# Two causal attentions: heads stacked on one set of 64 array rows instead of two row halves

## The chip, the cores and the metric

One core of a Trainium2 chip runs the whole program. TensorE (PE) multiplies, VectorE (DVE) reduces and copies, ScalarE (ACT) exponentiates, GpSimd (POOL) masks and issues the loads, SyncE (SP) issues stores. The metric is the device time of one execution in microseconds (us); lower is better. The kernel before took 5852.48 us (median of three runs, 5826.07 to 5913.86).

## The reference

Two layers over a (2, 2048, 256) input, each "x = layernorm(x + block(x))": a causal grouped attention (16 heads of 16 numbers, 4 key/value heads), a top-2 mixture of 8 experts, an attention with low-rank keys and values and rotary positions (16 heads, masked by pages of 64), and a block of two local-attention layers with gated units. The part that matters is the softmax attention over all 2048 positions:

```python
att = jnp.einsum('bsgmd,btgd->bgmst', q, k) / scale
att = jnp.where(causal, -jnp.inf, att)
att = jax.nn.softmax(att, axis=-1)
ctx = jnp.einsum('bgmst,btgd->bsgmd', att, v).reshape(b, s, DIM)
```

The second global attention computes the same with its own keys for each head and with `pages[None, :] <= pages[:, None]` as the mask.

## The kernel before, in words

The program runs stages one after another, named by the first letter of their tiles: Z clears buffers, A projects, **B is the first global attention**, C its output, then routing and E the experts, F combines and projects, **G is the second global attention** and H its output, and I, J, K are the local layers, each run twice. One function, `attention`, makes both B and G.

`attention` runs 8 iterations (2 batches of 4 groups); an iteration handles 4 heads. Queries and keys are kept split into a high and a low part, so that a product of 16 numbers keeps its precision: in `qs` and `ks` each head has three groups of 16 rows (high times high, low times high, high times low), 48 rows in all. Heads 0 and 2 lie in rows 0 to 47 and heads 1 and 3 in rows 64 to 111, that is, in the two halves of the array's 128 rows. Two more rows (48, 49 and 112, 113) hold the negated row maximum, split high and low, against ones in `ks`.

Each iteration does two things, interleaved:

- **Pieces** (line 419): for a block of 128 queries the scores against up to 512 keys are made in one of three PSUM buffers `pm` (RING), and DVE takes their maximum (509). On the diagonal a matmul against a mask (415) comes first. When the pieces of a chunk of 512 queries are done, DVE folds the maxima (515), POOL splits them in two (328, 330), PE turns them (409), ACT negates them (483), and SP writes them by DMA into `qs` (354). There are 144 pieces, in 160 matmuls.
- **Steps** (40 in an iteration, for 4 chunks of 512 queries by 128 keys each): four score matmuls (458) in two pairs, heads 0 and 1 and heads 2 and 3, over 48 + 2 rows; ACT takes the exponential of each pair (495); POOL masks on the diagonal (303); and PE weights the values of the step before with it (435), four heads side by side in 32 columns each.

The queues' order is written out by hand: the list `ring` holds pieces, folds and turns in order, `cut` deals some 3.8 of its events to each step, 22 steps ahead of the scores that need them (AHEAD), and the rest, 83 events, comes as an opening before the first iteration. In a step PE runs score pair 1, an event, score pair 2, an event, the weighting of the step before, and the other events. POOL loads the next iteration's `qs`, `ks` and `v` at step 4 (290 to 292).

Of the kernel before, what the change touches and what calls it, by code (L numbers as in the profile page):

```python
# [6 lines left out]
F32 = mybir.dt.float32  # L7
F32R = mybir.dt.float32r
# [169 lines left out]

def attention(nc, sem, tag, nk, page, qh, ql, kh, kl, vs, mask_qk, ident_bf, ident, ot):

    R = 3 * HD
    PAR = GRP // 2
    NA = max(1, nk // 2)
    RING = 3
    AHEAD = 22

# [5 lines left out]
    for qb in range(NQ):  # L192
        full, rest = divmod((qb + 1) * P, CH)
        for kc in range(full + (rest > CH // 2)):
            pieces += [(qb, kc, min(CH, (qb + 1) * P - kc * CH), [h]) for h in range(GRP)]
        if 0 < rest <= CH // 2:
            pieces += [(qb, full, rest, [u, u + 2]) for u in range(2)]
    NP = len(pieces)
    steps = [(qc, kb) for qc in range(NC4) for kb in range(SUB * (qc + 1))]
    NS = len(steps)  # L200
# [1 line left out]
    ring = []  # L202
    for j in range(NP):
        ring.append(("piece", j, 0))
        for behind, kind in ((1, "fold"), (4, "turn")):
            for c in range(NC4):
                if (closes[c] + behind) % NP == j:
                    ring.append((kind, c, (closes[c] + behind) // NP))
# [16 lines left out]

    with ExitStack() as ctx:
        sb = lambda n, s, t: ctx.enter_context(nc.sbuf_tensor(tag + n, s, t))
        qs = [sb(f"qs{i}", [P, NC4, PAR, CH], F32R) for i in range(2)]
        ks = [sb(f"ks{i}", [P, NA, S], F32R) for i in range(2)]
        v = [sb(f"v{i}", [P, NQ, nk, VW], F32) for i in range(2)]  # L230
        p = sb("p", [P, 2, GRP, CH], F32)
        o = sb("o", [P, 2, CH], F32)
        mpart = sb("mpart", [P, 2, PAR, NQ, NC4], F32)
        mfold = sb("mfold", [P, 2, PAR, SUB], F32)
        m = sb("m", [P, P], F32R)
        mrow = sb("mrow", [2 * GRP * SUB, P], F32)
        one = sb("one", [2, CH], F32)
# [20 lines left out]

            return sum(kb >= SUB * qc for qc, kb in steps[:t])

        LOADS = 2 * 6 + 1
        CONSTS = 3 + 4

        def all_iterations(eng, body):

# [11 lines left out]
        def _(pool):  # L277
# [3 lines left out]
            pool.dma_start(idf[:], ident).then_inc(c_in, 16)  # L281

            def load(i, s):
                q_rows = lambda a: a[ds(i * (GRP * HD), GRP * HD), :].rearrange("(a b e) (c t) -> b e c a t", b=2, e=HD, t=CH)
                k_rows = lambda a, u: (a[ds(i * HD, HD), :].unsqueeze(1) if nk == 1 else
                                       a[ds(i * (GRP * HD), GRP * HD), :].rearrange("(a b e) t -> b e a t", b=2, e=HD)[u])
                for u in range(2):
                    for r, (a, c) in enumerate(((qh, kh), (ql, kh), (qh, kl))):
                        rows = slice(64 * u + r * HD, 64 * u + (r + 1) * HD)
                        pool.dma_start(qs[s][rows].bitcast(F32), q_rows(a)[u]).then_inc(q_in[s], 16)  # L290
                        pool.dma_start(ks[s][rows].bitcast(F32), k_rows(c, u)).then_inc(q_in[s], 16)
                pool.dma_start(v[s][:], vs[ds(i * S, S), :].rearrange("(kb p) (h e) -> p kb h e", p=P, e=VW)
                               ).then_inc(q_in[s], 16)

# [15 lines left out]
            load(0, 0)  # L310
            pool.wait_ge(ready, 2)
            for s in range(2):
                for u in range(2):
                    pool.dma_start(ks[s][64 * u + R:64 * u + R + 2].bitcast(F32).rearrange("r a (c t) -> r (a c) t", t=CH),
                                   one[:].unsqueeze(1).to_broadcast([2, NA * NC4, CH])).then_inc(c_in, 16)
            load(1, 1)

            def split(k, e, clears):
                kind, c, late = ring[e]
                if kind != "fold":  # L320
                    return
                if clears is not None:
                    wait_apart(pool, cleared, clears, fence)
                wait_apart(pool, folded, (k - late) * NC4 + c + 1, fence)
                wait_apart(pool, mt_done, (k - late) * NC4 + c, fence)
                parts = m[:, 0:2 * GRP * SUB].rearrange("p (b r n) -> p r b n", b=2, r=2)
                whole = mfold[:].rearrange("p b a j -> p b (a j)")
# [19 lines left out]
        @block.sync  # L347
        def _(sp):
            def m_row(k, e, s):
                _, c, late = ring[e]  # L350
                sp.wait_ge(mr_done, (k - late) * NC4 + c + 2)
                s = (s + late) % 2
                for u in range(2):
                    sp.dma_start(qs[s][64 * u + R:64 * u + R + 2, c].bitcast(F32).rearrange("r a (j t) -> r (a j) t", t=P),
                                 mrow[u * GRP * SUB:(u + 1) * GRP * SUB]).then_inc(m_in, 16)

            def out(i, c):
                sp.wait_ge(o_done, i * NC4 + c + 2)
                sp.dma_start(ot[ds(i * P, P), c * CH:(c + 1) * CH], o[:, c % 2]).then_inc(o_out[c % 2], 16)

            for k, e in opening:
                if ring[e][0] == "turn":
                    m_row(k, e, 0)

            def body(i, s, half):
                for t, (qc, kb) in enumerate(steps):
                    for e in range(cut[t], cut[t + 1]):
                        if ring[e % NE][0] == "turn" and exists(i + e // NE, e % NE):
                            m_row(i + e // NE, e % NE, (s + e // NE) % 2)
                    if kb == 0:  # L370
                        if qc:
                            out(i, qc - 1)
                        elif not static(i, 0):
                            out(i - 1, NC4 - 1)
            all_iterations(sp, body)
            out(NIT - 1, NC4 - 1)
            for c in range(2):
                sp.wait_ge(o_out[c], 16 * (NC4 // 2 * NIT) + 1)

        @block.tensor  # L380
        def _(pe):
# [19 lines left out]
            def event(k, e, s):  # L401
# [13 lines left out]
                    pe.matmul(t[:, 0:c * w].rearrange("p (h k) -> p h k", k=w)[:, :, w - P:w], idb[:],  # L415
                              mqk[:].unsqueeze(1).to_broadcast([P, c, P]), start=True, stop=False, skip_group_check=True)
                for n, h in enumerate(heads):
                    rows = slice(64 * (h % 2), 64 * (h % 2) + R)
                    last = pe.matmul(t[:, n * w:(n + 1) * w],  # L419
                                     qs[s][rows, qb // SUB, h // 2, qb % SUB * P:(qb % SUB + 1) * P],  # L420
                                     ks[s][rows, h // 2 % NA, kc * CH:kc * CH + w], start=not diag, stop=True,
                                     skip_group_check=diag)
                last.then_inc(s_max, 1)

# [15 lines left out]
            def body(i, s, half):  # L440
                for t, (qc, kb) in enumerate(steps):
                    off = max(0, kb - SUB * qc) * P
                    events = [(e // NE, e % NE) for e in range(cut[t], cut[t + 1]) if exists(i + e // NE, e % NE)]
                    if kb == 0:
                        pe.wait_ge(m_in, (i * NC4 + qc + 1) * 32 + 1)

                    def some(a, z):
                        for n in range(a, min(z, len(events))):
# [5 lines left out]
                    for pr in range(2):  # L454
                        pe.wait_ge(e_done[pr], i * NS + t + 1)
                        for h in (2 * pr, 2 * pr + 1):
                            rows = slice(64 * (h % 2), 64 * (h % 2) + R + 2)
                            score = pe.matmul(psc[:, h, off:CH], ks[s][rows, h // 2 % NA, kb * P:(kb + 1) * P],  # L458
                                              qs[s][rows, qc, h // 2, off:CH], start=True, stop=True)
                        score.then_inc(s_done, 1)  # L460
                        some(pr, pr + 1)
                    if t:
                        weigh(i, s, t - 1)
                    elif not static(i, 0):
                        weigh(i - 1, 1 - s, NS - 1)
                    some(2, len(events))

            pe.wait_ge(c_in, 16 * CONSTS)
            pe.wait_ge(q_in[0], 16 * LOADS)
# [6 lines left out]
        def _(act):  # L476
            def m_rows(k, e):
                kind, c, late = ring[e]
                if kind != "turn":
                    return  # L480
                act.wait_ge(mt_done, (k - late) * NC4 + c + 2)
                act.wait_ge(m_in, (k - late) * (NC4 * 32) + c * 32 + 1)
# [19 lines left out]
        def _(dve):  # L502
            def event(k, e):
                kind, j, late = ring[e]
                if kind == "piece":
                    qb, kc, w, heads = pieces[j]
                    dve.wait_ge(s_max, k * NP + j + 2)
                    a = heads[0] // 2
                    dve.tensor_reduce(mpart[:, heads[0] % 2, a:a + len(heads), qb, kc],  # L509
                                      pm[slots[e]][:, 0:len(heads) * w].rearrange("p (h k) -> p h k", k=w),  # L510
                                      AX, ALU.max).then_inc(max_done, 1)
                elif kind == "fold":
                    dve.wait_ge(max_done, (k - late) * NP + closes[j] + 2)
                    dve.wait_ge(m_all, (k - late) * NC4 + j + 1)
                    dve.tensor_reduce(mfold[:].rearrange("p b a j -> p (b a) j"),
                                      mpart[:, :, :, j * SUB:(j + 1) * SUB].rearrange("p b a q k -> p (b a) q k"),
                                      AX, ALU.max).then_inc(folded, 1)

            def copy_out(i, qc):
# [1824 lines left out]
```

## Time and profile before

| | |
|---|---|
| median of 3 runs (lowest, highest) | 5852.48 us (5826.07, 5913.86) |
| profiled execution, its own time | 5825.77 us |
| its span, mean granted clock | 5824.2 us, 0.851 |
| B, from PE's first instruction to its last | 149.6 to 1187.3, 1037.7 us |
| G, likewise | 2553.3 to 3620.5, 1067.2 us |

The engines overlap, so busy shares do not add up. A matmul's recorded time holds its latency, so two that follow each other overlap in the record; how fast they follow is read from the difference of their starts. Two matmuls whose starts lie 0.004 us apart run side by side. The granted clock, PEclk, is a share of 2.4 GHz: 1.00 is that level, 0.50 is 1.2 GHz, and what lies between is a mean over both.

### The profile page before, as it was taken

To read this page: it belongs to the slowest core of one execution; us is meant where nothing else is said; L and a number is where in the kernel's file an instruction comes from. 1 tells how busy PE (TensorE), PEld (TensorE's weight loads), DVE (VectorE), ACT (ScalarE), POOL (GpSimd) and SP (SyncE) were. 2 spreads that over 40 slices of the span, in tenths; PEclk is the share of its full clock that TensorE was granted. 3 is DMA by queue.
4 is the path that set the end of the run, shared out by engine and by line. 5 is a ranking of instruction groups with operands and counts; after the bars stand their busy time and mean duration, and the time that the engine had idled before them with its cause. 6 is when DMAs were issued, how large, how long until landed. Compare 5 with 4: busy or idle time off the path is not lost. (4 is left out here: it accounts for less than half of the span.)

```text
span 5824.2 us, 81282 instructions
## 1 busy us (share of the span) xinstructions
PE 4707.0 (81%) x25828; PEld 3020.7 (52%) x25828; DVE 3059.5 (53%) x5338; ACT 2344.9 (40%) x3695; POOL 861.0 (15%) x1228
## 2 busy tenths in 40 slices
PE   4999999952999993759999998476997967699787
PEld 2444434341887882323434343355775755577566
DVE  1777767632344442746667674475443547444354
ACT  1365555521344441204555555133443423334333
POOL 1011211115000004010111110132111003211100
PEclk8698889875999996856778898698998989899888
DMA  7111221023112112350333220334332123333211
GB/s 213 25 27 27 35 40 29 11 96 114 48 47 75 46 44 85 130 103 9 49 47 50 38 40 22 120 118 133 111 118 78 33 60 118 125 118 110 73 43 33
DMA packets 271929, 413.90 MB, mean 71 GB/s; under 512 B 40836, under 2 KB 178945, under 8 KB 268028
## 3 DMA queue, kind: packets, MB, share of 16 engines
q0 software_dynamic: 64160, 224.28, 16.3%
q1 hardware_dynamic: 202844, 181.40, 9.7%
q8 instruction: 173, 2.83, 0.2%
q10 hardware_dynamic: 4608, 4.20, 0.2%
q14 instruction: 144, 1.18, 0.1%
HBM read 252.70 MB, written 156.19 MB: 70 GB/s over the span
## 5 line engine op out<-in xcount | busy, mean ns | idle before, releaser
L509 DVE TENSOR_REDUCE G_mpart<-G_pm 128x1 f32<-128x512 f32 (+3 forms) x1152 | 705.1, 656 | 340.3 <-PE G_pm L419 331.0
L509 DVE TENSOR_REDUCE B_mpart<-B_pm 128x1 f32<-128x512 f32 (+3 forms) x1152 | 704.4, 656 | 300.0 <-PE B_pm L419 290.4
L495 ACT ACTIVATE G_p<-G_psc 128x1024 f32<-128x1024 f32 (+3 forms) x640 | 544.1, 894 | 470.5 <-PE G_psc L458 469.7
L495 ACT ACTIVATE B_p<-B_psc 128x1024 f32<-128x1024 f32 (+3 forms) x640 | 543.1, 894 | 445.2 <-PE B_psc L458 444.6
L419 PE MATMUL G_pm<-G_ks,G_qs 48*128 48x512 f32 (+3 forms) x1280 | 523.5, 521 | 8.9 <-DVE G_mpart L509 4.3
L419 PE MATMUL B_pm<-B_ks,B_qs 48*128 48x512 f32 (+3 forms) x1280 | 510.3, 507 | 9.4 <-DVE B_mpart L509 4.1
L458 PE MATMUL G_psc<-G_qs,G_ks 50*128 50x512 f32 (+3 forms) x1280 | 357.9, 453 | 16.0 <-issue 13.4
L419 PEld LDWEIGHTS G_pm<-G_ks,G_qs 48*128 48x128 f32 x1280 | 231.4, 224 | 265.1 <-DVE G_mpart L509 171.4
L435 PE MATMUL G_po<-G_p,G_v 128*32 128x512 f32 (+3 forms) x2560 | 359.4, 639 | 6.7 <-DVE G_o L523 6.0
L419 PEld LDWEIGHTS B_pm<-B_ks,B_qs 48*128 48x128 f32 x1280 | 226.2, 218 | 259.3 <-DVE B_mpart L509 175.0
L458 PE MATMUL B_psc<-B_qs,B_ks 50*128 50x512 f32 (+3 forms) x1280 | 347.3, 440 | 10.0 <-issue 7.4
L435 PE MATMUL B_po<-B_p,B_v 128*32 128x512 f32 (+3 forms) x2560 | 348.1, 620 | 8.4 <-DVE B_o L523 6.6
L1017 PE MATMUL E_pO<-E_wp,E_a 128*128 128x256 f32 (+1 forms) x1920 | 255.2, 298 | 57.9 <-DVE E_a L1079 52.3
L1050 ACT ACTIVATE E_hs<-E_pH,E_bf 128x512 f32<-128x512 f32 (+1 forms) x192 | 115.7, 602 | 434.9 <-PE E_pG L1004 434.9
L1818 DVE TENSOR_REDUCE J_mx<-J_pS 128x8 f32<-128x2048 f32 x64 | 146.7, 2292 | 262.2 <-PE J_pS L1710 262.2
L1017 PEld LDWEIGHTS E_pO<-E_wp,E_a 128*128 128x128 f32 (+1 forms) x1920 | 250.0, 200 | 63.1 <-DVE E_a L1079 57.2
L1004 PE MATMUL E_pH<-E_xT,E_wfg 128*128 128x512 f32 (+1 forms) x1152 | 259.7, 362 | 19.7 <-DVE E_wfg L1089 15.6
L1004 PE MATMUL E_pG<-E_xT,E_wfg 128*128 128x512 f32 (+1 forms) x1152 | 255.1, 357 | 0.0
L1564 POOL TENSOR_TENSOR I_t<-I_qn,I_R 128x512 f32<-128x512 f32 x128 | 167.8, 1332 | 510.5 <-DVE I_qn L1618 510.5
L1726 PEld LDWEIGHTS J_pO<-J_v,J_pT 128*128 128x128 f32 x2048 | 239.6, 193 | 3.2
L1726 PE MATMUL J_pO<-J_v,J_pT 128*128 128x65 f32 x2048 | 236.5, 274 | 0.0
L1004 PEld LDWEIGHTS E_pH<-E_xT,E_wfg 128*128 128x128 f32 x1152 | 195.6, 193 | 55.4 <-issue 21.8
(308 smaller groups left out, 7879.6 us busy)
## 6 DMA issues: line engine op xcount, KB each, us to landing
J_v<-lve POOLq DMA_DIRECT2D x64, 520.0 KB, 4.2
J_k<-lkT POOLq DMA_DIRECT2D x64, 512.0 KB, 5.1
lve<-I_v SPq DMA_DIRECT2D x64, 260.0 KB, 2.1
lqT<-I_tT SPq DMA_DIRECT2D x64, 256.0 KB, 2.4
lkT<-I_tT SPq DMA_DIRECT2D x64, 256.0 KB, 2.6
J_q<-lqT POOLq DMA_DIRECT2D x64, 256.0 KB, 4.2
ein<-Z_z SPq DMA_DIRECT2D x8, 1228.0 KB
E_xin<-ein POOLq DMA_DIRECT2D x8, 1152.0 KB, 6.4
```

The lines of the kernel that those rows point to most:

```text
L419: last = pe.matmul(t[:, n * w:(n + 1) * w], qs[s][rows, qb // SUB, h // 2, qb % SUB * P:(qb % SUB + 1) * P], ks[s][rows, h // 2 % NA, kc * ...
L435: last = pe.matmul(po[VW * h:VW * (h + 1), off:CH], v[s][:, kb, h % nk], p[:, t % 2, h, off:CH], start=kb == 0, stop=kb == SUB * (qc + 1) - 1,
L458: score = pe.matmul(psc[:, h, off:CH], ks[s][rows, h // 2 % NA, kb * P:(kb + 1) * P], qs[s][rows, qc, h // 2, off:CH], start=True, stop=True)
L495: act.activation(p[:, t % 2, 2 * pr:2 * pr + 2, off:CH], psc[:, 2 * pr:2 * pr + 2, off:CH], ACT.Exp, scale=SC).then_inc(e_done[pr], 1)
L509: dve.tensor_reduce(mpart[:, heads[0] % 2, a:a + len(heads), qb, kc], pm[slots[e]][:, 0:len(heads) * w].rearrange("p (h k) -> p h k", k=w) ...
L1004: last = pe.matmul(bank[ht % 2][:, 0:w], wfg_p[pw][:, i, kc, ht * P:(ht + 1) * P], xT[px][:, kc, 0:w], start=kc + j == 0, stop=kc == KC - ...
L1017: last = pe.matmul(pO[j // 2][0:r, j % 2 * D:(j % 2 + 1) * D], a[pa][:, ht, j * P:j * P + r], wp_p[pw][:, ht], start=ht + i == 0, stop=ht ...
L1050: act.activation(hs[:, ht % 2, 0:w], pH[ht % 2][:, 0:w], ACT.Identity, bias=bf[:, s, ht:ht + 1]).then_inc(hs_done, 1)
L1564: last = pool.tensor_tensor(t2[:, u, :, :, a:a + H], qn[:, u, :, :, z:z + H], R[:, :, ds(w_, 1), a:a + H].to_broadcast([P, 2, LH, H]), ALU ...
L1726: last = pe.matmul(pO[h // HB][:, h % HB * VE:(h % HB + 1) * VE], pT[:, r, i, s], v[:, u, s, h * VE:(h + 1) * VE], start=s == 0, stop=s == 1)
L1818: dve.tensor_reduce(mx[:, u], pS[:], AX, ALU.max).then_inc(m_done, 1)
```

## The change

All four products of the split halves are now stacked, high-high, high-low, low-high and low-low, in 64 rows, and every head uses rows 0 to 63 of the array. The maximum's two rows are 64 and 65, so a score matmul reads rows 0 to 65. Pieces that hold two heads take neighbours (0 and 1, 2 and 3). The turn of the maxima comes 12 pieces after its chunk's last piece, not 4. In a step the weighting follows score pair 2 directly, and the event that stood there comes behind it. An iteration's load is 21 DMAs instead of 13, and the maxima are written by one DMA instead of two. Semaphore counts follow.

```diff
-    R = 3 * HD
-    PAR = GRP // 2
-    NA = max(1, nk // 2)
+    R = 4 * HD
...
-            pieces += [(qb, full, rest, [u, u + 2]) for u in range(2)]
+            pieces += [(qb, full, rest, [u, u + 1]) for u in (0, 2)]
...
-        for behind, kind in ((1, "fold"), (4, "turn")):
+        for behind, kind in ((1, "fold"), (12, "turn")):
...
-                for u in range(2):
-                    for r, (a, c) in enumerate(((qh, kh), (ql, kh), (qh, kl))):
-                        rows = slice(64 * u + r * HD, 64 * u + (r + 1) * HD)
-                        pool.dma_start(qs[s][rows].bitcast(F32), q_rows(a)[u]).then_inc(q_in[s], 16)
-                        pool.dma_start(ks[s][rows].bitcast(F32), k_rows(c, u)).then_inc(q_in[s], 16)
+                for r, (a, c) in enumerate(((qh, kh), (qh, kl), (ql, kh), (ql, kl))):
+                    rows = slice(r * HD, (r + 1) * HD)
+                    for h in range(GRP):
+                        pool.dma_start(qs[s][rows, :, h].bitcast(F32), a[ds(i * (GRP * HD) + h * HD, HD), :]
+                                       .rearrange("e (c t) -> e c t", t=CH)).then_inc(q_in[s], 16)
+                    pool.dma_start(ks[s][rows].bitcast(F32), c[ds(i * (nk * HD), nk * HD), :].rearrange("(h e) t -> e h t", e=HD)
+                                   ).then_inc(q_in[s], 16)
...
-                for u in range(2):
-                    sp.dma_start(qs[s][64 * u + R:64 * u + R + 2, c].bitcast(F32).rearrange("r a (j t) -> r (a j) t", t=P),
-                                 mrow[u * GRP * SUB:(u + 1) * GRP * SUB]).then_inc(m_in, 16)
+                sp.dma_start(qs[s][R:R + 2, c].bitcast(F32).rearrange("r a (j t) -> r (a j) t", t=P),
+                             mrow[:]).then_inc(m_in, 16)
...
-                    rows = slice(64 * (h % 2), 64 * (h % 2) + R)
                     last = pe.matmul(t[:, n * w:(n + 1) * w],
-                                     qs[s][rows, qb // SUB, h // 2, qb % SUB * P:(qb % SUB + 1) * P],
-                                     ks[s][rows, h // 2 % NA, kc * CH:kc * CH + w], start=not diag, stop=True,
+                                     qs[s][0:R, qb // SUB, h, qb % SUB * P:(qb % SUB + 1) * P],
+                                     ks[s][0:R, h % nk, kc * CH:kc * CH + w], start=not diag, stop=True,
...
-                            rows = slice(64 * (h % 2), 64 * (h % 2) + R + 2)
-                            score = pe.matmul(psc[:, h, off:CH], ks[s][rows, h // 2 % NA, kb * P:(kb + 1) * P],
-                                              qs[s][rows, qc, h // 2, off:CH], start=True, stop=True)
+                            score = pe.matmul(psc[:, h, off:CH], ks[s][0:R + 2, h % nk, kb * P:(kb + 1) * P],
+                                              qs[s][0:R + 2, qc, h, off:CH], start=True, stop=True)
                         score.then_inc(s_done, 1)
-                        some(pr, pr + 1)
+                        if pr == 0:
+                            some(0, 1)
...
-                    some(2, len(events))
+                    some(1, len(events))
```

What PE runs in one step of stage B in which nothing is masked, before (458 scores, 419 pieces, 435 weighting; the number behind a tile is its buffer):

```order
L458 MATMUL B_psc<-B_qs0,B_ks0 128x512 x2
L419 MATMUL B_pm2<-B_ks0,B_qs0 128x512
L458 MATMUL B_psc<-B_qs0,B_ks0 128x512 x2
L419 MATMUL B_pm0<-B_ks0,B_qs0 128x512
L435 MATMUL B_po<-B_p,B_v0 32x512 x4
```

and in such a step now (451 scores, 413 pieces, 429 weighting):

```order
L451 MATMUL B_psc<-B_qs0,B_ks0 128x512 x2
L413 MATMUL B_pm1<-B_ks0,B_qs0 128x512
L451 MATMUL B_psc<-B_qs0,B_ks0 128x512 x2
L429 MATMUL B_po<-B_p,B_v0 32x128 x4
L413 MATMUL B_pm2<-B_ks0,B_qs0 128x512
L413 MATMUL B_pm0<-B_ks0,B_qs0 128x512
L413 MATMUL B_pm1<-B_ks0,B_qs0 128x512
```

The instructions are the same in number and size; the piece ahead of the weighting has moved behind it, and three now stand there in a row. Not in these rows: before, neighbours took the array's two halves in turn, and now all take its lower rows.

The load that POOL issues for one iteration, at the start of stage B, before:

```order
L290 DMA B_qs<-qh 16x8x512
L291 DMA B_ks<-kh 16x2048
L290 DMA B_qs<-ql 16x8x512
L291 DMA B_ks<-kh 16x2048
L290 DMA B_qs<-qh 16x8x512
L291 DMA B_ks<-kl 16x2048
L290 DMA B_qs<-qh 16x8x512
L291 DMA B_ks<-kh 16x2048
L290 DMA B_qs<-ql 16x8x512
L291 DMA B_ks<-kh 16x2048
L290 DMA B_qs<-qh 16x8x512
L291 DMA B_ks<-kl 16x2048
```

and now:

```order
L285 DMA B_qs<-qh 16x4x512 x4
L287 DMA B_ks<-kh 16x2048
L285 DMA B_qs<-qh 16x4x512 x4
L287 DMA B_ks<-kl 16x2048
L285 DMA B_qs<-ql 16x4x512 x4
L287 DMA B_ks<-kh 16x2048
L285 DMA B_qs<-ql 16x4x512 x4
L287 DMA B_ks<-kl 16x2048
L289 DMA B_v<-vs 128x16x32
```

Queries come head by head, half as much in each DMA, and a fourth product is loaded; the load of `v` follows in both.

## Rows read from the trace of the kernel before

**Rows 1.** The page: span, engine totals, and PE's busy tenths and clock in 40 slices

```profile
span 5824.2 us, 81282 instructions
PE 4707.0 (81%) x25828; PEld 3020.7 (52%) x25828; DVE 3059.5 (53%) x5338; ACT 2344.9 (40%) x3695; POOL 861.0 (15%) x1228
PE   4999999952999993759999998476997967699787
PEclk8698889875999996856778898698998989899888
```

**Rows 2.** Busy time of each engine, clock, DMA: stages B and G, first to last PE instruction

```profile
149.60:1187.30 1037.70, 989.58 (x5536) 417.20 (x5536) 723.45 (x1216) 548.81 (x672) 140.62 (x270) 0.83 0.17 27
2553.30:3620.50 1067.20, 1019.61 (x5536) 428.44 (x5536) 724.25 (x1216) 551.11 (x673) 98.47 (x270) 0.80 0.23 37
```

**Rows 3.** Who waited for whom: us in total, times, longest us

```profile
ACT B_p L495 <- PE B_psc L458: 444.6, 346, 21.3
DVE B_mpart L509 <- PE B_pm L419: 290.4, 354, 29.2
PE B_pm L409 <- POOL B_m L330: 11.4, 10, 1.3
PE G_pm L409 <- POOL G_m L330: 8.8, 10, 1.2
```

**Rows 4.** Timeline of PE in stage B at the full clock: start, us, instruction, count

```profile
806.08 0.51 PE L419 MATMUL B_pm<-B_ks,B_qs 48*128 48x512 f32 x2
806.43 0.63 PE L458 MATMUL B_psc<-B_qs,B_ks 50*128 50x512 f32 x4
806.90 0.40 PE L419 MATMUL B_pm<-B_ks,B_qs 48*128 48x512 f32 x1
807.23 1.06 PE L435 MATMUL B_po<-B_p,B_v 128*32 128x512 f32 x8
808.22 0.50 PE L419 MATMUL B_pm<-B_ks,B_qs 48*128 48x512 f32 x2
```

**Rows 5.** Timeline of PE in stage E (experts), all 128 rows, full clock

```profile
1644.50 1.56 PE L1004 MATMUL E_pH<-E_xT,E_wfg 128*128 128x512 f32 x6
1645.89 1.56 PE L1004 MATMUL E_pG<-E_xT,E_wfg 128*128 128x512 f32 x6
```

**Rows 6.** Timeline of PE in stage B at half the clock

```profile
787.36 0.63 PE L458 MATMUL B_psc<-B_qs,B_ks 50*128 50x512 f32 x2
787.92 0.40 PE L415 MATMUL B_pm<-B_mqk,B_idb 128*128 128x256 bf16 x1
788.24 0.58 PE L419 MATMUL B_pm<-B_ks,B_qs 48*128 48x256 f32 x1
...
790.45 1.93 PE L435 MATMUL B_po<-B_p,B_v 128*32 128x512 f32 x8
792.31 0.79 PE L419 MATMUL B_pm<-B_ks,B_qs 48*128 48x512 f32 x2
792.90 0.63 PE L458 MATMUL B_psc<-B_qs,B_ks 50*128 50x512 f32 x2
793.33 0.62 PE L419 MATMUL B_pm<-B_ks,B_qs 48*128 48x512 f32 x1
...
796.37 0.23 PE L415 MATMUL B_pm<-B_mqk,B_idb 128*128 128x128 bf16 x1
```

**Rows 7.** Busy times as in rows 2, of stretches at one clock each

```profile
149.60:198.00 48.40, 46.50 (x109) 22.51 (x109) 38.93 (x67) 0.53 (x2) 0.82 (x4) 0.50 0.40 46
198.00:230.00 32.00, 31.34 (x119) 14.00 (x122) 22.24 (x38) 10.96 (x15) 2.95 (x6) 0.50 0.03 9
776.00:782.50 6.50, 5.24 (x38) 2.32 (x36) 4.64 (x9) 2.81 (x6) 1.69 (x4) 1.00 0.01 3
792.00:796.20 4.20, 4.20 (x20) 1.64 (x16) 2.48 (x4) 1.94 (x2) 0.00 (x0) 0.50 0.02 4
806.00:826.00 20.00, 19.71 (x127) 8.31 (x127) 16.36 (x28) 14.60 (x17) 1.05 (x3) 1.00 0.01 2
```

**Rows 8.** POOL's timeline: a load in stage B, and the mask after it

```profile
851.15 0.58 POOL L290 DMA_DIRECT2D B_qs<-qh  x1 [0.20 <-issue]
851.77 0.51 POOL L291 DMA_DIRECT2D B_ks<-kh  x1
...
870.71 0.63 POOL L303 TENSOR_SCALAR_AFFINE_SELECT B_p<-B_p 128x512 f32<-128x512 f32 x1 [10.05 <-ACT B_p L495]
```

More of the change, by code:

```diff
@@ L227, in attention @@
         sb = lambda n, s, t: ctx.enter_context(nc.sbuf_tensor(tag + n, s, t))
-        qs = [sb(f"qs{i}", [P, NC4, PAR, CH], F32R) for i in range(2)]
-        ks = [sb(f"ks{i}", [P, NA, S], F32R) for i in range(2)]
+        qs = [sb(f"qs{i}", [P, NC4, GRP, CH], F32R) for i in range(2)]
+        ks = [sb(f"ks{i}", [P, nk, S], F32R) for i in range(2)]
         v = [sb(f"v{i}", [P, NQ, nk, VW], F32) for i in range(2)]
@@ L232, in attention @@
         o = sb("o", [P, 2, CH], F32)
-        mpart = sb("mpart", [P, 2, PAR, NQ, NC4], F32)
-        mfold = sb("mfold", [P, 2, PAR, SUB], F32)
+        mpart = sb("mpart", [P, GRP, NQ, NC4], F32)
+        mfold = sb("mfold", [P, GRP, SUB], F32)
         m = sb("m", [P, P], F32R)
@@ L259, in masked @@
             return sum(kb >= SUB * qc for qc, kb in steps[:t])
-        LOADS = 2 * 6 + 1
-        CONSTS = 3 + 4
+        LOADS = 4 * (GRP + 1) + 1
+        CONSTS = 3 + 2
         def all_iterations(eng, body):
@@ L283, in load @@
             def load(i, s):
-                q_rows = lambda a: a[ds(i * (GRP * HD), GRP * HD), :].rearrange("(a b e) (c t) -> b e c a t", b=2, e=HD, t=CH)
-                k_rows = lambda a, u: (a[ds(i * HD, HD), :].unsqueeze(1) if nk == 1 else
-                                       a[ds(i * (GRP * HD), GRP * HD), :].rearrange("(a b e) t -> b e a t", b=2, e=HD)[u])
-                for u in range(2):
-                    for r, (a, c) in enumerate(((qh, kh), (ql, kh), (qh, kl))):
-                        rows = slice(64 * u + r * HD, 64 * u + (r + 1) * HD)
-                        pool.dma_start(qs[s][rows].bitcast(F32), q_rows(a)[u]).then_inc(q_in[s], 16)
-                        pool.dma_start(ks[s][rows].bitcast(F32), k_rows(c, u)).then_inc(q_in[s], 16)
+                for r, (a, c) in enumerate(((qh, kh), (qh, kl), (ql, kh), (ql, kl))):
[5 more added lines that the diff above has]
+                                   ).then_inc(q_in[s], 16)
                 pool.dma_start(v[s][:], vs[ds(i * S, S), :].rearrange("(kb p) (h e) -> p kb h e", p=P, e=VW)
@@ L312, in _ @@
             for s in range(2):
-                for u in range(2):
-                    pool.dma_start(ks[s][64 * u + R:64 * u + R + 2].bitcast(F32).rearrange("r a (c t) -> r (a c) t", t=CH),
-                                   one[:].unsqueeze(1).to_broadcast([2, NA * NC4, CH])).then_inc(c_in, 16)
+                pool.dma_start(ks[s][R:R + 2].bitcast(F32).rearrange("r a (c t) -> r (a c) t", t=CH),
+                               one[:].unsqueeze(1).to_broadcast([2, nk * NC4, CH])).then_inc(c_in, 16)
             load(1, 1)
@@ L325, in split @@
                 wait_apart(pool, mt_done, (k - late) * NC4 + c, fence)
-                parts = m[:, 0:2 * GRP * SUB].rearrange("p (b r n) -> p r b n", b=2, r=2)
-                whole = mfold[:].rearrange("p b a j -> p b (a j)")
+                parts = m[:, 0:2 * GRP * SUB].rearrange("p (r n) -> p r n", r=2)
+                whole = mfold[:].rearrange("p a j -> p (a j)")
                 pool.tensor_copy(parts[:, 0], whole).then_inc(m_hi, 1)
@@ L352, in m_row @@
                 s = (s + late) % 2
-                for u in range(2):
-                    sp.dma_start(qs[s][64 * u + R:64 * u + R + 2, c].bitcast(F32).rearrange("r a (j t) -> r (a j) t", t=P),
-                                 mrow[u * GRP * SUB:(u + 1) * GRP * SUB]).then_inc(m_in, 16)
+                sp.dma_start(qs[s][R:R + 2, c].bitcast(F32).rearrange("r a (j t) -> r (a j) t", t=P),
+                             mrow[:]).then_inc(m_in, 16)
             def out(i, c):
@@ L444, in body @@
                     if kb == 0:
-                        pe.wait_ge(m_in, (i * NC4 + qc + 1) * 32 + 1)
+                        pe.wait_ge(m_in, (i * NC4 + qc + 1) * 16 + 1)
                     def some(a, z):
@@ L481, in m_rows @@
                 act.wait_ge(mt_done, (k - late) * NC4 + c + 2)
-                act.wait_ge(m_in, (k - late) * (NC4 * 32) + c * 32 + 1)
+                act.wait_ge(m_in, (k - late) * (NC4 * 16) + c * 16 + 1)
                 act.activation(mrow[:], pm[slots[e]][0:2 * GRP * SUB, 0:P], ACT.Copy, scale=-1.0).then_inc(mr_done, 1)
@@ L507, in event @@
                     dve.wait_ge(s_max, k * NP + j + 2)
-                    a = heads[0] // 2
-                    dve.tensor_reduce(mpart[:, heads[0] % 2, a:a + len(heads), qb, kc],
+                    dve.tensor_reduce(mpart[:, heads[0]:heads[-1] + 1, qb, kc],
                                       pm[slots[e]][:, 0:len(heads) * w].rearrange("p (h k) -> p h k", k=w),
@@ L514, in event @@
                     dve.wait_ge(m_all, (k - late) * NC4 + j + 1)
-                    dve.tensor_reduce(mfold[:].rearrange("p b a j -> p (b a) j"),
-                                      mpart[:, :, :, j * SUB:(j + 1) * SUB].rearrange("p b a q k -> p (b a) q k"),
+                    dve.tensor_reduce(mfold[:],
+                                      mpart[:, :, j * SUB:(j + 1) * SUB],
                                       AX, ALU.max).then_inc(folded, 1)
```

## The prediction

> **What bounds the kernel now.** I read the page first: PE is recorded busy for 81% of the span, more than any other engine, and its slices are nearly all 9s, while the clock row wanders between 5 and 9 [rows 1]. The change touches only the two global attentions, B and G, so the next view is the windows over them: 1037.7 and 1067.2 us, 2104.9 together, with PE in work for 95% of it, DVE for some 70%, ACT for 53%, at a mean clock of 0.83 and 0.80 [rows 2]. The waits say the same from the other side: ACT waits 444.6 us in B for scores from PE and DVE 290.4 us for pieces, while what PE itself waits for is small [rows 3]. So in B and G the end is set by how fast PE gets through its list, and that hangs on three things: whether matmuls run side by side, what a change of layout costs, and the clock.
>
> *Side by side.* At the full clock four score matmuls of 512 columns start at 806.43 and the next instruction at 806.90: 0.47 us for four, 0.235 for a pair [rows 4]. In E, where each uses all 128 rows, six take 1.39 us, 0.232 each [rows 5]. A pair in two row halves costs what one alone costs. The same holds for a piece beside a score of the other half.
>
> *Changes of layout.* I call it a change when PE goes from one way of using the array (a row half, all rows, four column strips) to another. Piece to weighting takes 0.33 (806.90 to 807.23), 0.10 over the plain 0.233; and the first pair behind a weighting takes 0.35 until the next, 0.115 more than a pair: its weights load in the open [rows 4]. At half the clock a pair takes 0.43 (792.90 to 793.33), scores to mask 0.56, so 0.13 for the change, and the first pair behind a weighting 0.59, so 0.16 for the weights [rows 6]. The weighting takes 0.99 to the next start at the full clock, 1.86 at half: 0.89 and 1.73 without its change [rows 4, 6].
>
> **What the edits cost.** The instructions stay the same. What goes is the pairing, and what comes is changes of layout: scores now read rows 0 to 65, across the half boundary, so I take them to use the array whole, as the mask matmuls do, while pieces on rows 0 to 63 remain a half. Counted over the program's order, one iteration of B has 167 changes before and 248 now; on 172 of them (76 into scores, 96 into pieces) a full set of weights loads in the open.
>
> Per iteration there are 28 steps with 512 columns and four each with 384, 256 and 128, which is 34 full ones: 136 full-size score matmuls, 136 piece matmuls (the same triangle), 34 weightings and 8192 mask columns. A mask of 256 columns takes 0.32 less 0.13 [rows 6], so these are 6.1 us at half the clock and about 3.0 at full.
>
> - At half the clock: 272 x 0.43 = 117.0; 34 x 1.73 = 58.8; masks 6.1; 248 x 0.13 = 32.2; 172 x 0.16 = 27.5. Sum 241.6, times 8 iterations 1933 us.
> - At the full clock: 272 x 0.233 = 63.4; 34 x 0.89 = 30.3; masks 3.0; 248 x 0.10 = 24.8; 172 x 0.115 = 19.8. Sum 141.3, times 8 is 1130, and 1150 with the opening at half the clock as now [rows 7].
>
> Both are above today's 1052 mean: the attentions get slower at either level, and the clock decides by how much. DVE (723 us) and ACT (549) fit under either sum [rows 2].
>
> **The clock.** In B it was at half for the opening and beyond, 149.6 to 230, though PE was in work for 46.5 of 48.4 and 31.3 of 32.0 us: busy alone did not bring it up [rows 7]. It fell after a thin stretch around a diagonal (776 to 782.5, narrow matmuls, PE in work for 5.24 of 6.50), and rose after 792 to 796.2, where two piece-score pairs, another pair and two weightings of 512 columns stood close [rows 6, 7]. What preceded the rise was the array in use in both halves at once, next to weightings that fill it. After the change nothing but masks, turns and weightings uses more than rows 0 to 65; at half the clock a full step becomes 8 x 0.43 + 1.73 + 5 x 0.13 + 4 x 0.16 = 6.5 us, with eight matmuls one by one, where it is 4.06 now (792.31 to 796.37). The thin stretches at the diagonals stay and get thinner. I conclude that the clock still falls, and that the stretches that raised it no longer exist: it stays at half nearly throughout. By the Trainium skill (TensorE: Matmul & The Clock Gate, "What's actually happening") sustained work releases the gate and only idleness closes it; by that rule the changed attentions would run at the full clock. Rows 7 speak against it for half-filled arrays.
>
> Each tenth of the work done at the full clock returns (1933 - 1130) / 10 = 80 us per attention. I take one tenth: 1853 us each. The bounds are none and three tenths.
>
> **The other edits.** The turn's later place removes at most the 11.4 and 8.8 us that PE waits for POOL there [rows 3]; I take all, -20. Its maxima are needed at steps 12 and 24 and turned at steps 5 and 21, the tightest with three steps to spare, some 10 us or more: no new wait. The piece behind the weighting costs no extra change; it is in the counts. Eight more loads at 0.55 us [rows 8] stand before PE's first instruction: 4.4 us each and some landing, +10 for both; zero and +40 are the bounds. Inside the iterations POOL issues 21 for 13, some 14 us for 9, with the next mask 19.6 us after the first issue today and later in a slower kernel [rows 8]: covered by four steps. Were the mask late all the same, it would be by 14 - 9 = 5 us at most, in 6 loads of each attention: 60 us, an upper bound. One DMA for the maxima instead of two saves SP 0.6 us off PE's path: nothing.
>
> Sum: 2 x 1853 - 2105 = +1601, -20, +10: +1591. Against the profiled execution's 5825.77 that is **7420 us**; the median of the runs shown is 27 above that execution, well inside my range.
>
> **The rivals.**
> - *The clock recovers in each iteration.* If undivided scores count like full-array work, stretches of scores next to a weighting can bring it up, and half the work runs fast: 1933 - 400 = 1530 each, in all 6770; with less of it up to 7250. For it speaks that E's work, on all rows, runs at the full clock [rows 5]; against it, that scores fill only 66 rows.
> - *The full clock throughout*, as in 806 to 826 today [rows 7]: 1150 each, +195 - 10, in all 6010. For it: PE gets denser in time, with no gaps. Against: the opening.
> - *Faster: changes cost nothing.* If rows 0 to 63 and rows 0 to 65 count as one layout and the full clock holds, only the 80 changes around weightings remain: 63.4 + 30.3 + 3.0 + 8.0 + 4.6 = 109.3, 895 per attention with the opening, in all 5510. It decides in step for step between scores and pieces: at full clock the kernel breaks even when a change with its weights costs 0.13 on average, and the rows give 0.10 + 0.115 x 172 / 248 = 0.18. The Trainium skill (TensorEngine Tiling (Array Packing), "Key Properties") says that changing the tiling mode drains TensorE, and the trace agrees with 0.10 to 0.13 [rows 4, 6]. At half the clock it would lose even with free changes: (117.0 + 58.8 + 6.1) x 8 = 1455.
>
> **Chances.** Half the clock nearly throughout 0.67 (7250 to 7600); recovering in part 0.15 (6650 to 7250); full clock 0.13; free changes 0.03; something between that ends within 2% 0.02. About 2% (117 us) is what the runs can tell from no change. The range 6650 to 7620 leaves out the last three. Faster 0.03, same 0.02, slower 0.95.
>
> **What would show it.** The changed profile should have B and G near 1850 us with a mean clock near 0.55 or less; scores of a pair 0.43 apart and not 0.004; 0.56 from a score pair to its piece; DVE and ACT with the same work over a longer time; turns without a wait for POOL; all other stages as long as now. I am wrong if the clock row shows 8s and 9s in B and G (then 6010), or if scores and pieces follow each other without the extra 0.1. Nothing here rests on other stages.

## The result, and the profile after

The changed kernel took 7660.23 us (median of four runs, 7629.05 to 7670.92) against 5853.6 before: a ratio of 1.3098, with a 95% interval of 1.303 to 1.3166. Forecast were 7420 and a range of 6650 to 7620. The direction and the mechanism held; the size was short by 240 us, and the time lies 40 above the range. Medians here are over all executions and ratios over the fast ones alone, which matters in experiment 3, where two of four were slow (6304.73, the profiled one, and 6376.31 us).

The page of the changed kernel, the lines that answer to [rows 1]:

```profile
span 7668.6 us, 81462 instructions
PE 6607.0 (86%) x25828; PEld 3738.6 (49%) x25828; DVE 3110.4 (41%) x5338; ACT 2400.7 (31%) x3695; POOL 917.2 (12%) x1352
PE   5999999999936999567999999999667979669967
PEclk7555555555568999785555555555688989879988
```

PE executes as many instructions as before. The clock row is a flat 5 over both attentions, slices 2 to 11 and 19 to 28, counted from 1. The windows over them, and over parts of them (columns as in [rows 2]):

```profile
151.20:2115.80 1964.60, 1961.25 (x5536) 780.74 (x5536) 748.27 (x1215) 577.08 (x672) 163.68 (x318) 0.50 0.10 15
3496.30:5441.30 1945.00, 1934.96 (x5536) 770.48 (x5536) 748.29 (x1216) 578.06 (x673) 121.47 (x318) 0.51 0.16 24
...
200.00:2115.80 1915.80, 1912.60 (x5428) 756.57 (x5427) 708.86 (x1148) 576.55 (x670) 162.85 (x314) 0.50 0.09 14
3496.30:5404.00 1907.70, 1898.59 (x5312) 756.88 (x5312) 747.58 (x1214) 547.96 (x637) 119.63 (x312) 0.50 0.17 24
5404.00:5441.30 37.30, 36.37 (x228) 13.60 (x224) 0.70 (x2) 30.10 (x36) 1.84 (x6) 1.00 0.02 9
```

B and G take 3909.6 us together where they took 2104.9 [rows 2]: +1805 of the span's +1844. From 200 us to the end of B PE is in work for 1912.6 of 1915.8 us, and its granted clock never leaves half. DVE and ACT do the same work as before, in busy times 3 to 5% longer. The clock comes up once, at 5404 in G, when no pieces are left; ahead of it the timeline of PE shows only scores, weightings and one turn:

```profile
5396.63 2.08 PE L451 MATMUL G_psc<-G_qs,G_ks 66*128 66x512 f32 x4
5398.64 1.94 PE L429 MATMUL G_po<-G_p,G_v 128*32 128x512 f32 x8
...
5402.30 1.94 PE L429 MATMUL G_po<-G_p,G_v 128*32 128x512 f32 x8
```

The missing pieces alone do not explain it: B's last piece starts by 2037, and the same scores and weightings to its end at 2115.8 stay at half the clock.

The waits, which answer to [rows 3] (who waited for whom: us, times, longest us):

```profile
ACT B_p L489 <- PE B_psc L451: 1309.3, 589, 17.0
DVE B_mpart L502 <- PE B_pm L413: 1163.6, 704, 30.6
```

Both engines wait for PE three to four times as long as before, and at the turns PE no longer waits for POOL: those lines are gone.

PE's timeline in stage B, at half the clock, which answers to [rows 6]:

```profile
1043.73 1.65 PE L413 MATMUL B_pm<-B_ks,B_qs 64*128 64x512 f32 x3
1045.30 1.22 PE L451 MATMUL B_psc<-B_qs,B_ks 66*128 66x512 f32 x2
1046.33 0.33 PE L410 MATMUL B_pm<-B_mqk,B_idb 128*128 128x128 bf16 x1
1046.59 0.79 PE L413 MATMUL B_pm<-B_ks,B_qs 64*128 64x512 f32 x1
1047.31 1.22 PE L451 MATMUL B_psc<-B_qs,B_ks 66*128 66x512 f32 x2
1048.46 1.94 PE L429 MATMUL B_po<-B_p,B_v 128*32 128x512 f32 x8
1050.33 0.29 PE L410 MATMUL B_pm<-B_mqk,B_idb 128*128 128x128 bf16 x1
```

Each price of the prediction can be read off it. Three pieces until the scores: 1.57, that is 3 x 0.43 + 0.16 + 0.13. Two scores until the mask: 1.03, that is 2 x 0.43 + 0.16, with no change between them, since both use the whole array. One piece until the scores: 0.72, that is 0.43 + 0.16 + 0.13. Two scores until the weighting: 1.15, 0.13 more than 1.02. The weighting: 1.87, as before. Nothing runs side by side.

### The profile page after: what moved, and what is told of

It reads as the page before. It is cut to its first block and busy times, and to the rows that moved or that the text cites. A ratio compares the mean times of both kernels' runs of the same rounds, so it can differ in the third digit from the quotient of the medians.

```text
span 7668.6 us, 81462 instructions
## 1 busy us (share of the span) xinstructions
PE 6607.0 (86%) x25828; PEld 3738.6 (49%) x25828; DVE 3110.4 (41%) x5338; ACT 2400.7 (31%) x3695; POOL 917.2 (12%) x1352
## 5 line engine op out<-in xcount | busy, mean ns | idle before, releaser
L413 PE MATMUL G_pm<-G_ks,G_qs 64*128 64x512 f32 (+3 forms) x1280 | 751.7, 670 | 0.2 <-DVE G_mpart L502 0.2
L413 PE MATMUL B_pm<-B_ks,B_qs 64*128 64x512 f32 (+3 forms) x1280 | 751.7, 670 | 0.1
L451 PE MATMUL B_psc<-B_qs,B_ks 66*128 66x512 f32 (+3 forms) x1280 | 689.4, 647 | 2.9 <-issue 2.9
L451 PE MATMUL G_psc<-G_qs,G_ks 66*128 66x512 f32 (+3 forms) x1280 | 676.8, 635 | 9.4 <-issue 8.9
L413 PEld LDWEIGHTS B_pm<-B_ks,B_qs 64*128 64x128 f32 x1280 | 343.6, 304 | 407.7 <-issue 267.3
L413 PEld LDWEIGHTS G_pm<-G_ks,G_qs 64*128 64x128 f32 x1280 | 343.6, 304 | 407.7 <-issue 267.3
L429 PE MATMUL B_po<-B_p,B_v 128*32 128x512 f32 (+3 forms) x2560 | 537.5, 933 | 0.3 <-POOL B_p L300 0.3
L429 PE MATMUL G_po<-G_p,G_v 128*32 128x512 f32 (+3 forms) x2560 | 523.6, 910 | 0.4 <-POOL G_p L304 0.3
L451 PEld LDWEIGHTS B_psc<-B_qs,B_ks 66*128 66x128 f32 x1280 | 322.7, 312 | 303.8 <-issue 294.7
L451 PEld LDWEIGHTS G_psc<-G_qs,G_ks 66*128 66x128 f32 x1280 | 313.3, 304 | 298.9 <-issue 276.2
```

The source lines that it names most:

```text
L413: last = pe.matmul(t[:, n * w:(n + 1) * w], qs[s][0:R, qb // SUB, h, qb % SUB * P:(qb % SUB + 1) * P], ks[s][0:R, h % nk, kc * CH:kc * CH ...
L429: last = pe.matmul(po[VW * h:VW * (h + 1), off:CH], v[s][:, kb, h % nk], p[:, t % 2, h, off:CH], start=kb == 0, stop=kb == SUB * (qc + 1) - 1,
L451: score = pe.matmul(psc[:, h, off:CH], ks[s][0:R + 2, h % nk, kb * P:(kb + 1) * P], qs[s][0:R + 2, qc, h, off:CH], start=True, stop=True)
```

## The experiments

All were timed against the kernel before on the same chip; a ratio is to that kernel. "B" and "G" are the two attentions' windows of the profiled execution, from PE's first instruction to its last.

**1. Filling the rows of the scores.** Two theories stood: that the clock stays down because matmuls that run one by one fill half the rows (theory 1), or because of the rhythm with its pauses at 248 changes of layout (theory 2). Edit on the changed kernel:

```diff
+            for t in (*qs, *ks):
+                dve.memset(t[64:P].bitcast(F32), 0.0)
...
-                            score = pe.matmul(psc[:, h, off:CH], ks[s][0:R + 2, h % nk, kb * P:(kb + 1) * P],
-                                              qs[s][0:R + 2, qc, h, off:CH], start=True, stop=True)
+                            score = pe.matmul(psc[:, h, off:CH], ks[s][:, h % nk, kb * P:(kb + 1) * P],
+                                              qs[s][:, qc, h, off:CH], start=True, stop=True)
```

> The changed kernel with one thing added: rows 66 to 127 of the query and key tiles hold zeros, and a score matmul reads all 128 rows instead of 66. The instructions, their columns, their order and their layouts (scores over the whole array, pieces over a half) stay the same, and so does the result. In the changed kernel's profile both attentions run at half the clock from end to end (mean 0.50), 1965 and 1945 us. Theory 1 (rows in use): the clock stays down because scores and pieces go one by one and fill half of the array's rows. Then filling the rows of the scores alone brings the clock up for most of B and G, to 0.85 or more, and each takes 1150 to 1300 us: in all 6150 to 6400. Theory 2 (rhythm): the clock stays down because of the pauses at the many changes of layout, whatever rows are filled. Then nothing moves: clock 0.50 and 7660 within 1%.

Measured: 6208.09 us, ratio 1.0645 (1.056 to 1.073). The windows over B and G:

```profile
151.50:1370.30 1218.80, 1206.05 (x5536) 516.69 (x5536) 721.82 (x1215) 575.88 (x672) 168.36 (x326) 0.92 0.16 24
2726.10:3964.80 1238.70, 1210.46 (x5536) 517.39 (x5536) 722.47 (x1215) 577.14 (x673) 121.49 (x318) 0.91 0.26 37
```

Multiplying zeros brought the clock from 0.50 to 0.92 and took 1452 us off B and G. The order, the columns and the 248 changes stayed. Theory 1 holds; rhythm alone does not keep the clock down. This kernel's timeline also shows the changes' price at the full clock:

```profile
806.44 0.97 PE L413 MATMUL B_pm<-B_ks,B_qs 64*128 64x512 f32 x3
807.34 0.73 PE L451 MATMUL B_psc<-B_qs,B_ks 128*128 128x512 f32 x2
808.00 0.50 PE L413 MATMUL B_pm<-B_ks,B_qs 64*128 64x512 f32 x1
808.43 0.73 PE L451 MATMUL B_psc<-B_qs,B_ks 128*128 128x512 f32 x2
```

Three pieces until the scores take 0.90, two scores until the piece 0.66, one piece until the scores 0.43. Less 0.233 for each matmul, a change with its weights costs 0.19 to 0.20, where the prediction had 0.10 + 0.115.

**2. Three products in the lower half.** Edit: `R = 3 * HD`, three of the four products in the load, `LOADS = 3 * (GRP + 1) + 1`.

> The changed kernel with three split products again (48 rows, and 50 with the maximum) but all heads in the lower rows, so that scores and pieces both use the lower half: nothing is paired, and the changes of layout between scores and pieces are gone (some 168 per iteration as before the change, not 248). It leaves out the low-low product. If the cost at half the clock is what I summed, an iteration takes 117.0 + 58.8 + 6.1 + 168 x 0.13 + 77 x 0.16 = 216 us, an attention 1727, and the whole 7200. If the clock theory of rows in use holds it stays at 0.50, since still fewer rows are filled. If instead the changes of layout held the clock down (theory 2), the clock comes back towards 0.8 and the whole is under 6700.

Measured: 7248.64 us, ratio 1.2409 (1.231 to 1.2507).

```profile
144.50:1910.80 1766.30, 1761.51 (x5536) 830.00 (x5536) 745.75 (x1215) 576.28 (x672) 148.09 (x288) 0.50 0.09 14
3257.20:5028.50 1771.30, 1761.40 (x5536) 830.02 (x5536) 745.75 (x1215) 577.56 (x673) 105.97 (x288) 0.50 0.14 22
```

With 80 changes of layout fewer the clock is still 0.50, so theory 2 falls here too. B is 198 us shorter than in the changed kernel; the rows' prices give (80 x 0.13 + 95 x 0.16) x 8 = 205. G is 174 shorter, against a G whose last 37 us ran at the full clock.

**3. The two small edits alone, on the kernel before** (turn 12 behind, weighting directly behind score pair 2):

```diff
-        for behind, kind in ((1, "fold"), (4, "turn")):
+        for behind, kind in ((1, "fold"), (12, "turn")):
...
-                        some(pr, pr + 1)
+                        if pr == 0:
+                            some(0, 1)
...
-                    some(2, len(events))
+                    some(1, len(events))
```

> The kernel before with the two small edits alone: the turn of the maxima 12 pieces behind and the weighting directly behind score pair 2; heads stay in two row halves. In the prediction these were worth -20 us (the waits for POOL at the turn) and nothing for the moved piece. Rival: the moved piece loses a partner, since a piece between pair 2 and the weighting ran beside a score of the other half; then a few pieces more run alone, 40 iterations' steps x 16 x up to 0.2 us, up to +130 us. I expect between -20 and +60: 5830 to 5910.

Measured: 6260.2 us, ratio 1.06 (1.0475 to 1.0724): far outside the 5830 to 5910 expected. The clock in B and G of the profiled execution was 0.66 and 0.60, where it is 0.83 and 0.80 before. Experiments 4 and 5 part the two edits.

**4. The turn alone**, on the kernel before: the first line pair of the diff above.

> The kernel before with the turn of the maxima 12 pieces behind instead of 4, and nothing else. The two small edits together cost 6% on the kernel before, where I had expected at most 60 us; one of the two must have done it. Theory A (the moved piece): the turn is harmless, -20 to +20 us, 5836 to 5876, clock over 0.8. Theory B (the turn): it does it, for the pieces' buffers are held by a turn at another place, and the time is near 6200.

Measured: 5862.57 us, ratio 0.9979 (0.9936 to 1.0023): no change, theory A. In its profiled execution, at 5904.09 us one of its slowest, the clock was 0.83 in B and, below the 0.8 expected, 0.75 in G.

**5. The order alone**, on the kernel before: the rest of that diff.

> The kernel before with the weighting directly behind score pair 2, and the turn where it was. Theory A (the moved piece): ahead of the weighting the piece ran beside a score of the other half; behind it, of three pieces one more stays alone, so the half-clock stretches last longer and the clock stays down: near 6200, clock in the attentions near 0.63. Theory B (the turn): under 5880.

Measured: 6398.72 us, ratio 1.094 (1.087 to 1.1011).

```profile
149.00:1462.40 1313.40, 1266.05 (x5536) 488.39 (x5536) 723.96 (x1215) 564.29 (x672) 140.61 (x270) 0.62 0.13 21
2812.00:4159.40 1347.40, 1301.84 (x5536) 500.03 (x5536) 725.22 (x1215) 566.70 (x673) 98.48 (x270) 0.59 0.18 29
```

The order does it, and through the clock: by the clock's records in the traces, B and G are at half the clock for 2111 of their 2661 us, before for 768 of 2105. As an estimate, at 0.235 us for a pair at the full clock and 0.43 at half, 1343 us more at half are worth some 600, and B and G grew by 556. PE's timeline in this kernel's stage B has a piece without a partner behind the weighting:

```profile
805.06 1.94 PE L435 MATMUL B_po<-B_p,B_v 128*32 128x512 f32 x8
806.93 0.79 PE L419 MATMUL B_pm<-B_ks,B_qs 48*128 48x512 f32 x1
807.65 0.29 PE L415 MATMUL B_pm<-B_mqk,B_idb 128*128 128x128 bf16 x1
```

It takes 0.72 us until the mask, with half of the array idle. But the kernel before has the same ahead of the weighting:

```profile
793.89 0.79 PE L419 MATMUL B_pm<-B_ks,B_qs 48*128 48x512 f32 x1
794.61 1.83 PE L435 MATMUL B_po<-B_p,B_v 128*32 128x512 f32 x8
```

Counted over all of B in the traces (an estimate that lets each matmul stream one column per clock from its start), 36% of the columns of scores and pieces run alone before and 35% here; in the stretches at half the clock 28% and 34%. There are 1342 changes of layout in both. So the order costs the clock, but that it does so by parting pairs is not shown, and why it does stays open. Nor was it settled why both edits together (1.06) cost less than the order alone (1.094), while the turn alone costs nothing.

**6. The old order in the changed kernel.** Edit: the reverse of the order edit.

> The changed kernel (all heads in the lower rows, turn 12 behind) with the old order of a step: one piece between score pair 2 and the weighting. On the row halves the new order cost 9%, since the moved piece lost its partner in the other half. Here nothing has a partner, so that cannot happen: the clock stays at 0.50, and the piece between scores and weighting adds one change of layout with its weights per step, 0.13 + 0.16 less the change from scores to weighting that it replaces, 40 x 0.2 x 8 x 2 = up to 100 us: 7660 to 7770. If the order acted through something else than pairs, this would be much faster than 7660.

Measured: 7739.97 us, ratio 1.3174 (1.3076 to 1.3273), against 1.3098 (1.303 to 1.3166) for the changed kernel; B and G at clock 0.50, 2009 and 2015 us, 44 and 70 more in the profiled execution. The intervals overlap, so the two kernels cannot be told apart by their times. The trace counts 2047 changes of layout in B where the changed kernel has 1955: the new order costs no extra change, as the prediction had it. A clock that is at half already could not fall, so this does not say what experiment 5 lost.

**7. One layout for all.** Zeros in rows 64 to 125, the maximum's rows at 126 and 127. Edit on the changed kernel, with the memset of experiment 1:

```diff
-                                     qs[s][0:R, qb // SUB, h, qb % SUB * P:(qb % SUB + 1) * P],
-                                     ks[s][0:R, h % nk, kc * CH:kc * CH + w], start=not diag, stop=True,
+                                     qs[s][0:P - 2, qb // SUB, h, qb % SUB * P:(qb % SUB + 1) * P],
+                                     ks[s][0:P - 2, h % nk, kc * CH:kc * CH + w], start=not diag, stop=True,
...
-                            score = pe.matmul(psc[:, h, off:CH], ks[s][0:R + 2, h % nk, kb * P:(kb + 1) * P],
-                                              qs[s][0:R + 2, qc, h, off:CH], start=True, stop=True)
+                            score = pe.matmul(psc[:, h, off:CH], ks[s][:, h % nk, kb * P:(kb + 1) * P],
+                                              qs[s][:, qc, h, off:CH], start=True, stop=True)
```

> The changed kernel with all matmuls of scores and pieces over the whole array: zeros in rows 64 to 125, the maximum's two rows at 126 and 127, pieces read rows 0 to 125 and scores all. Nothing is paired, but scores, pieces, masks and turns share one layout, and only the weighting changes it (80 changes per iteration). The result stays the same. Theory 1 says that the clock is up from the first steps to the end (over 0.95 behind the opening), and the sum of the prediction's third rival applies: 109.3 us an iteration, 895 us an attention if PE alone sets the pace, up to 980 with waits for DVE, so 5450 to 5730 in all, faster than both kernels. Theory 2 (rhythm) agrees on the clock here, for it too has few changes left. If the clock stays at 0.50 both are wrong, and the time is 5826 - 2105 + 2 x 1500 = 6720.

Measured: 5765.91 us, ratio 0.9869 (0.9791 to 0.9947).

```profile
150.40:1145.00 994.60, 946.43 (x5536) 484.71 (x5536) 708.53 (x1215) 553.19 (x672) 168.46 (x326) 0.99 0.20 30
2505.40:3547.40 1042.00, 959.99 (x5536) 492.05 (x5536) 709.00 (x1215) 554.94 (x673) 121.56 (x318) 0.96 0.31 44
```

The clock is up as expected. Against experiment 1, 168 changes an iteration are gone, and B and G are 224 and 197 us shorter, 0.17 and 0.15 us for each change. That is no clean price: the clock rose as well, from 0.92 to 0.99 and from 0.91 to 0.96, and PE's time without work grew from 13 to 48 and from 28 to 82 us. The attentions are longer than the 895 to 980 expected, and the whole than 5450 to 5730: the sum for PE alone left out the turns and the waits. PE waits 31 us in B and 29 in G for DVE, most of it for the copy of the output, and 25 in G for the DMA of the maxima.

**8. One layout, old order.** The reverse of the order edit on experiment 7.

> The one-layout kernel (all scores and pieces over all 128 rows) with the old order of a step: one piece between score pair 2 and the weighting. There are no pairs to lose here and the number of layout changes is the same, 80 an iteration. A piece ahead of the weighting gives VectorE its work earlier, and its maximum is taken while PE weights. If the attentions there wait for VectorE in between, this is 20 to 60 us faster than the one-layout kernel (5766): 5700 to 5745. If PE alone sets the pace it is the same within 10 us.

Measured: 5698.95 us, ratio 0.9739 (0.9693 to 0.9785); B 961.4 us, G 1012.1. Some 30 us less in each. The waits of PE's weighting for DVE's copy of the output go from 23.9 to 9.3 us in B and from 21.9 to 8.7 in G, which fits the expectation that a piece ahead of the weighting supplies DVE sooner.

**9. Filled rows in the two halves.** Edit on the kernel before (its loads wait for the zeros, and the maximum's rows move to 62 and 63 of each half):

```diff
-            dve.memset(one[:], 1.0).then_inc(ready, 1)
+            dve.memset(one[:], 1.0)
+            for i in range(2):
+                dve.memset(qs[i][:].bitcast(F32), 0.0)
+                dve.memset(ks[i][:].bitcast(F32), 0.0).then_inc(ready, 1)
...
-                    rows = slice(64 * (h % 2), 64 * (h % 2) + R)
+                    rows = slice(64 * (h % 2), 64 * (h % 2) + 62)
...
-                            rows = slice(64 * (h % 2), 64 * (h % 2) + R + 2)
+                            rows = slice(64 * (h % 2), 64 * (h % 2) + 64)
```

> The kernel before (two row halves, its own order and turn) with its rows filled: zeros in rows 48 to 61 of each half, the maximum's two rows at 62 and 63, pieces read 62 rows of a half instead of 48 and scores 64 instead of 50. The result stays the same, and so do instructions, order, pairs and layouts; the zeros are written once at the start of each attention, some 15 us. If rows in use decide the clock, it rises from 0.83 and 0.80 to over 0.88 in both attentions, and each takes 60 to 100 us less than 1037 and 1067: 5670 to 5740 in all. If the pauses decide it, the clock stays at 0.82 and the time is 5856 plus up to 20.

Measured: 5687.21 us, ratio 0.972 (0.967 to 0.977).

```profile
155.60:1150.20 994.60, 941.16 (x5536) 399.04 (x5536) 719.78 (x1215) 548.51 (x672) 140.77 (x270) 0.89 0.18 28
2507.10:3478.20 971.10, 916.56 (x5536) 390.10 (x5536) 718.17 (x1215) 549.70 (x673) 98.48 (x270) 0.92 0.25 40
```

The only thing that PE does differently is to multiply 14 more rows of zeros in each half. The clock goes from 0.83 and 0.80 to 0.89 and 0.92, and B and G are 43 and 96 us shorter, where 60 to 100 each was expected.

**10. The same with whole pairs of pieces**: no event between the score pairs, two ahead of the weighting.

```diff
-                        some(pr, pr + 1)
+                        if pr == 1:
+                            some(0, 2)
```

> The padded row halves (5687 us) with the events of a step dealt in pairs: none between the score pairs, two between score pair 2 and the weighting, the rest behind it, so that neighbouring pieces of the two halves meet. If pairing and the clock are what counts, more pieces have a partner, the clock in the attentions goes over 0.92, and each attention takes 20 to 50 us less: 5590 to 5650. If VectorE's three buffers set the pace there, PE waits for them ahead of the weighting and it is the same or slower: 5690 or more.

Measured: 5693.4 us, ratio 0.9708 (0.9656 to 0.9761). B and G at 0.91 and 0.94 take 978.9 and 957.1 us, 16 and 14 less than in experiment 9, where 20 to 50 was expected, but the whole is the same: in its profiled execution the other stages took 63 us more (3756.7 against 3693.9). Such stages have the same code in both kernels, so this is how much they wander. The edit hardly made pairs: counted as in experiment 5, 37 to 38% of the columns run alone, 38 to 39% in experiment 9.

Experiments 8, 9 and 10 beat both kernels and cannot be told from one another.

## Why the prediction was wrong

**What bounds the kernel** was read rightly: PE's list sets the end of B and G, before and after. DVE, ACT, the three buffers and the later turn played no part: from 200 us to B's end PE waits 3.2 us in all.

**Side by side and changes of layout**: right in kind and price. Each price at half the clock is found again in the timeline above, and experiment 2 removed changes in B for what the rows of the kernel before said, within 4%. At the full clock the timeline of experiment 1 has them some 10% cheaper than the rows did. That scores on rows 0 to 65 use the array whole and pieces on rows 0 to 63 half of it was an assumption; the missing change between scores and mask, and the change between pieces and scores, confirm it.

**The clock**: the mechanism is right, and experiment 1 shows it: 1452 of the 1805 us that B and G lost come back when zeros fill the rows of the scores. Experiment 7 takes another 421 with the changes of layout and the clock that rose with it. What is left is 68 us below the kernel before: running one by one at 0.97 of the clock, with 80 changes an iteration, is slightly cheaper than running in pairs at 0.82 with 167. Rows in use are not the whole of it: experiment 5 has the same rows, columns and number of changes as the kernel before, and its clock is 0.60.

**The step that failed** is the line "I take one tenth: 1853 us each". It mis-sized how much of the work would still be done at the full clock, and took 160 us off the forecast. It was nothing in B and 37 us at the very end of G. I had argued that the stretches which raised the clock no longer exist and then granted a tenth back without a row for it. With none, the sum gives 2 x 1933 - 2105 = +1761, and with -20 and +10 the whole comes to 7577.

**What then remains** is 93 us of the profiled execution's 7670, enough to pass the upper end. Of these, 44 are the sum at half the clock: 1933 for measured 1965 and 1945. It did not price the 32 turns of each attention (9 us by the differences of their starts) nor the loops' ends, where PE stands for 2.9 us in B and 8.9 in G; the rest, about 1% of the sum, stays open. Another 20 are the turns' waits, which were not to be had twice: the sum by rows contained no such waits in the first place. The other 30 lie outside B and G: they took 40 us more where I had 10. G's first instruction waited 11 us longer for the bigger load, B's came 1.6 later, and what follows G took 24 more, within what such stages wander. The upper end of 7620 was the sum's "none" case with 43 us to spare; it gave the sum itself no error, and 2% of 3900 us is 78.

**The small edits**: "the piece behind the weighting costs no extra change" is true of the kernel it was written for (experiment 6), and the turn is free (experiment 4). On the row halves the same move costs 9% (experiment 5), which my expectation for experiment 3 missed by some 300 us: I priced it in columns and not in clock.

**The rivals**: "the full clock throughout" rested on PE's being busy without gaps. It was, for 99.8% of B from 200 us on, and the clock stayed at half. "Changes cost nothing" failed by the timeline. The partly recovering clock came true only where experiment 1 filled the rows.

## What to carry to other kernels

A TensorE that is recorded busy for the whole of a stage may still run it at half the clock: read the granted clock beside the busy share, and ask how many of the array's rows each matmul fills. Where a contraction is short, either put different heads into different row groups and fill the rows that remain with zeros, which cost no column and here gave 2.8% (experiment 9), or run each over all rows, filled with zeros, in one layout; both came to a ratio of 0.97. Time the order of the matmuls too, for it can move the clock. When a bound of a sum is its most favourable or its least favourable case, give the sum its own error on top.

## What the runs showed of the hardware that was not expected

- Rows of zeros count: with 66 rows the scores' clock was 0.50, with the same matmuls on 128 rows, 62 of them zero, 0.92 (experiment 1); with 62 and 64 rows of each half instead of 48 and 50 it went from 0.83 and 0.80 to 0.89 and 0.92 (experiment 9).
- Being busy did not raise the clock: the changed kernel had PE in work for 1912.6 of 1915.8 us of B, matmuls one by one on 64 and 66 rows, without one rise.
- Moving one matmul per step from one side of the weighting to the other moved the mean clock from 0.82 to 0.60 and the time by 9% (experiment 5), with no instruction and no change of layout added.
